# A four-layer transformer block on one core: the last layer's expert rows by inverted lists, its shared experts evicted by ScalarE and GpSimd, its experts chosen in turn

## What is computed

```python
def _gate(x2d, gate_w, gate_bias):                # E=16, K=4, G=4 groups, TG=2
    scores = jax.nn.sigmoid(x2d @ gate_w.T)
    sfc = scores + gate_bias[None, :]
    top2, _ = jax.lax.top_k(sfc.reshape(T, G, E // G), 2)
    _, gidx = jax.lax.top_k(top2.sum(-1), TG)     # the two best groups
    gmask = jnp.zeros((T, G), sfc.dtype).at[jnp.arange(T)[:, None], gidx].set(1.0)
    tmp = jnp.where(jnp.repeat(gmask, E // G, axis=1) > 0, sfc, 0.0)
    _, topk_idx = jax.lax.top_k(tmp, K)
    topk_w = jnp.take_along_axis(scores, topk_idx, axis=1)
    return (topk_idx, topk_w / (topk_w.sum(-1, keepdims=True) + 1e-20))
...
g = jnp.einsum('th,eih->tei', x, gate_proj)       # I=352 hidden units an expert
u = jnp.einsum('th,eih->tei', x, up_proj)
y = jnp.einsum('tei,ehi,te->th', jax.nn.silu(g) * u, down_proj, combine_w)
y = y + jax.nn.silu(x @ shared_gate_w.T) * (x @ shared_up_w.T) @ shared_down_w.T   # 2 x 352 units
...
x = x + jnp.tanh(g_ffn[3]) * _L3_ffn_ref(_layernorm(x, axis=-1), ...)
```

## Time and profile before

| | |
|---|---|
| median of 3 runs | 2774.49 us (2771.5 to 2775.27) |
| the profiled execution | 2772.54 us, its span 2770.7 us |
| mean granted TensorE clock | 0.927 |
| TensorE busy | 2361.6 us (85%) |
| VectorE busy | 1306.6 us (47%) |
| ScalarE busy | 890.4 us (32%) |
| GpSimd busy | 664.1 us (24%) |

### The profile page before, as it was taken

How to read it: one execution, slowest core, us unless ns; L and a number is a source line. 1 busy time by engine, 2 the same in 40 slices (tenths; PEclk the granted TensorE clock), 3 DMA queues, 4 the chain that set the end, 5 groups by cost and what they waited for, 6 DMA issues and landing times. The chain is left out here.

```text
span 2770.7 us, 31859 instructions
## 1 busy us (share of the span) xinstructions
PE 2361.6 (85%) x11410; PEld 1572.0 (57%) x11410; DVE 1306.6 (47%) x2786; ACT 890.4 (32%) x1996; POOL 664.1 (24%) x751
## 2 busy tenths in 40 slices
PE   6898978879688759996899989999988647999995
PEld 3454654546447647775444555444556524888873
DVE  5766256662646631112667445567444551333325
ACT  3444235452243222221456323465322110111110
POOL 3034231212202112221100122100121035332346
PEclk9989989999789779998999999999999668999997
DMA  9000000000000322221000000000000032666633
GB/s 361 2 1 1 0 1 1 1 1 1 8 0 22 134 94 99 97 96 64 1 16 1 1 1 0 1 1 1 1 1 1 0 122 97 217 222 232 224 129 117
DMA packets 59109, 164.13 MB, mean 59 GB/s; under 512 B 6529, under 2 KB 41089, under 8 KB 50913
## 3 DMA queue, kind: packets, MB, share of 16 engines
q0 software_dynamic: 20032, 90.00, 9.3%
q1 hardware_dynamic: 38960, 72.59, 7.5%
HBM read 119.84 MB, written 42.73 MB: 59 GB/s over the span
## 5 line engine op out<-in xcount | busy, mean ns | idle before, releaser
L646 ACT ACTIVATE arena<-PS,arena 128x512 f32<-128x512 f32 (+3 forms) x512 | 305.7, 605 | 202.6 <-DVE arena L689 172.2
L689 DVE TENSOR_REDUCE arena<-PS 128x1 f32<-128x512 f32 (+3 forms) x512 | 273.0, 583 | 136.0 <-PE PS L591 84.9
L585 PE MATMUL PS<-arena 64*128 64x512 f32 (+3 forms) x1024 | 292.7, 564 | 31.8 <-ACT arena L646 21.3
L297 POOL TENSOR_TENSOR arena<-arena 128x4 f32<-128x4 f32 x41 | 47.0, 1145 | 754.7 <-DVE arena L308 440.8
L2312 PE MATMUL PS<-arena 128*128 128x256 f32 (+2 forms) x1128 | 215.9, 348 | 0.9 <-DVE arena L2357 0.9
L2312 PEld LDWEIGHTS PS<-arena 128*128 128x128 f32 (+1 forms) x1128 | 182.3, 183 | 28.9 <-issue 1.3
L585 PEld LDWEIGHTS PS<-arena 64*128 64x128 f32 x1024 | 103.6, 186 | 144.0 <-ACT arena L646 95.6
L615 PE MATMUL PS<-arena 128*128 128x128 f32 x1280 | 170.7, 278 | 15.7 <-ACT arena L646 12.8
L870 POOL TENSOR_TENSOR arena<-arena 128x512 f32<-128x512 f32 (+2 forms) x108 | 88.8, 825 | 381.8 <-ACT arena L841 376.2
L615 PEld LDWEIGHTS PS<-arena 128*128 128x128 f32 x1280 | 137.4, 141 | 69.4 <-ACT arena L646 48.0
L982 PE MATMUL PS<-arena 128*128 128x512 f32 x384 | 168.0, 594 | 3.1 <-ACT arena L999 3.1
(11 more groups left out here) (395 smaller groups left out, 3932.4 us busy)
## 6 DMA issues: line engine op xcount, KB each, us to landing
arena<-e SPq DMA_DIRECT2D x8, 2048.0 KB, 8.6
slots<-zeros SPq DMA_DIRECT2D x1, 10112.0 KB, 60.8
arena<-slots SPq DMA_DIRECT2D x32, 256.0 KB, 3.3
yslots<-arena POOLq DMA_DIRECT2D x32, 256.0 KB, 2.6
arena<-w3a SPq DMA_DIRECT2D x1, 4106.0 KB, 13.6
yslots<-zeros SPq DMA_DIRECT2D x1, 4096.0 KB, 32.9
arena<-w3b SPq DMA_DIRECT2D x1, 3593.0 KB, 20.2
arena<-yslots SPq DMA_DIRECT2D x6, 512.0 KB, 5.8
```

What stands on the lines that cost most here:

```text
L585: ins = nc.tensor.matmul(PS[:, hh, 0:w], q[:, t * P:(t + 1) * P], k[:, 0:w], start=True, stop=not cfg["causal"])
L646: nc.scalar.activation(PRB[m % 6][:, 0:w], PS[:, hh, 0:w], ACT.Exp, bias=nmax[:, m:m + 1], accum_out=rsum[:, col:col + 1]).then_inc(s["pro ...
L689: nc.vector.tensor_reduce(nmax[:, m:m + 1], PS[:, hh, 0:w], AX, ALU.max, negate=True).then_inc(s["nmax"], 1)
```

## The change

It has five parts.

1. **Experts are chosen in turn.** `dve_take` replaces `dve_rank` for the experts of both mixtures: it takes the largest score (the first of equals), writes its one-hot mask, lowers it by a large number and goes on. That is six operations on 256 elements for each of the four choices (128 elements and two choices in the third layer). The mask of chosen experts is bf16.
2. **Places by products alone.** `pe_positions` lets TensorE add up the tiles before, with bf16 tables of ones (`ones16`, `upto16`); the running sums on VectorE are gone, in both mixtures.
3. **The fourth layer gets inverse lists** as the third has: one-hot rows of 64 x 79 and 64 x 128 elements (`dve_onehots3`), 64 products (`pe_rows3`) and `dve_rows3`. GpSimd gathers each tile of rows from the tokens by `from_row3` and stores each tile of outputs by `to_row3`; SyncE keeps the normalised tokens in `slots3`, reads a batch's expert number from `weight_row3` into a register and loads the weights by a plain DMA, and reads the outputs back by 16 plain DMAs. The 64 scatters, the 64 gathers and the 10 MB of zeros are gone.
4. **Shared experts** leave VectorE. ScalarE does silu and copies the up part and, scaled, the down part out of PSUM; GpSimd multiplies and adds to x. Gate and up of the next block stand ahead of the down products of a block. Half 0 starts when the scores are copied, and the two sets of products of the routing stand within it, behind its first and its last block; half 1 stays behind the batches. Its last four additions wait until VectorE has combined everything (`summed`), and the combining of a quarter waits for GpSimd's additions (`added`).
5. **The third layer's routing** also hands one multiplication of its one-hot rows to GpSimd (`pool_onehots`), and TensorE adds the parts for the second list. Empty slots read a row of zeros in `slots2`.

```diff
+            for k, (pick, top) in enumerate(zip(picks, tops)):
+                ch.link(v.tensor_reduce(top, val, AX, ALU.max))
+                ch.link(v.tensor_tensor(key, val, over(top), ALU.is_equal))
+                ch.link(v.scalar_tensor_tensor(out=key, in0=place, scalar=-float(P), in1=key, op0=ALU.add, op1=ALU.mult))
+                ch.link(v.tensor_reduce(least, key, AX, ALU.min))
+                ins = v.tensor_tensor(pick, key, over(least), ALU.is_equal)
...
+                ch.link(v.scalar_tensor_tensor(out=val, in0=pick, scalar=NEG, in1=val, op0=ALU.mult, op1=ALU.add))
...
+        def pool_onehots(highs, n, nh, signal):
+
+            for k in range(n // NT):
+                ins = nc.gpsimd.tensor_tensor(highs[:, k * NT:(k + 1) * NT, 0, :], highs[:, k * NT:(k + 1) * NT, 2, :],
+                                              counting[:, 1:NT + 1].unsqueeze(2).to_broadcast([P, NT, nh]), ALU.mult)
+            ins.then_inc(signal, 1)
+
+        def pe_positions(to, chosen, n, e):
+
+            for d in range(n):
+                ins = nc.tensor.matmul(to[:, d * e:n * e], ones16[:, :] if d else upto16[:, :], chosen[:, 0:(n - d) * e],
+                                       start=d == 0, stop=d == n - 1)
...
-            rank = temp(NT * E3).rearrange("p (t e) -> p t e", e=E3)
-            dve_rank(ch, sfc, rank, E3)
...
+            dve_take(ch, sfc, [onehot[:, k] for k in range(TOPK3)], TOPK3 * [top], E3)
...
-            V.tensor_copy(slot_of3[:, :], slot).then_inc(s["slots"], 1)
+            nseg = TOPK3 * NT
+            high, low = temp(nseg), temp(nseg)
+            dve_floor(ch, high, slot, P)
+            ch.link(V.scalar_tensor_tensor(out=low, in0=high, scalar=-float(P), in1=slot, op0=ALU.mult, op1=ALU.add))
+            dve_onehots3(ch, low3, high3, low, high, nseg, HI3, s["tables"])
...
             V.tensor_copy(weight_row3[:, :], row_).then_inc(s["slots"], 1)
+            v.wait_ge(s["table_psum"], 2)
+            dve_rows3(ch, PS[:, 3, 300:300 + 2 * HI3], HI3, TOPK3 * NT * P, from_row3[:, :], to_row3[:, :], temp,
+                      s["slots"])
...
+        def pool_mix3(pool, it, c):
+            n = IC3[c]
+            pool.wait_ge(s3m["up_out"], it * 6 + 2 * c + 2)
+            to = mixed3[it % 2][c][0:n, :]
+            nc.gpsimd.tensor_tensor(to, to, ups3[(it * 3 + c) % 2][0:n, :], ALU.mult).then_inc(s3m["mixed"], 1)
+
+        def pool_add3(pool, it):
+            for t in range(QT):
+                pool.wait_ge(s3m["down_out"], it * QT + t + 1)
+                xt = X[:, it % B * QT + t, :]
+                nc.gpsimd.tensor_tensor(xt, xt, downs3[t], ALU.add).then_inc(s3m["added"], 1)
...
+            for j in range(NB3):
+                jj, i = divmod(j, 3)
+                j_ = batch_expert(jj, i)
+                first = sp.value_load(weight_row3[0:1, j_:j_ + 1], min_val=0, max_val=(E3 - 1) * P)
+                if j >= 3:
+                    sp.wait_ge(s["o_psum"], j - 2)
+                elif j == 1:
+                    sp.wait_ge(s2m["kept"], KEPT2 + 32)
+                sp.dma_start(wbuf3[i], e3_in.rearrange("e p n -> (e p) n")[bass.ds(first, P), :]).then_inc(s[f"w{i}"], 16)
...
+            for q in range(B):
+                for k in range(TOPK3):
+                    sp.dma_start(yk3[:, k, q * QT:(q + 1) * QT, :], kept_rows(yslots3, k * NT + q * QT, QT)
+                                 ).then_inc(BACK3[q][0], 16)
...
             for q in range(B):
-                v.wait_ge(s[f"gathered{q}"], TOPK3 * QT * 16)
+                v.wait_ge(BACK3[q][0], BACK3[q][1] + TOPK3 * 16)
+                if q < B - 1:
+                    v.wait_ge(s["added"], (B + q + 1) * QT)
+                else:
+                    v.wait_ge(s["added"], B * QT)
...
+            def rows(j):
+                jj, i = divmod(j, 3)
+                if j >= 3:
+                    pool.wait_ge(s["xT_psum"], j - 2)
+                for t, n in enumerate(batch_tiles(jj, i)):
...
+            def store(j):
+                jj, i = divmod(j, 3)
+                pool.wait_ge(s["copied"], j + 4)
...
+            for j in range(NB3):
+                store(j)
+                if j + 3 < NB3:
+                    rows(j + 3)
+
+            def before_last():
+                pool.wait_ge(s["summed"], B * TOPK3)
+            pool_shared3(pool, 1, before_last)
...
-            sp.dma_start(slots3[0:ROWS3, :].rearrange("(t p) c -> p t c", p=P),
-                         zeros[:, :].unsqueeze(1).to_broadcast([P, ROWS3 // P, C])).then_inc(ld["zeroed"], 16)
```

More of the change, by code:

```diff
@@ L1624, in program @@
                    "y1_stored first back0 back1 back2 wa wb act_in hidden o_psum")
[L1625 to L1626 removed]
+        s3m = sems("l3moe", "sig tables table_psum slots x0 x1 x2 w0 w1 w2 xT_psum xT copied y0_stored y1_stored "
+                   "y2_stored back3 wa act_in dve_in hidden o_psum extra up_psum up_out mixed down down_out added summed")
         gtile = hT.rearrange("p a n -> p (a n)")
@@ new lines, in pool_shared3 @@
+        def pool_shared3(pool, i, last):
+            for b in range(B):
+                it = i * B + b
+                pool_mix3(pool, it, 0)
+                if b:
+                    pool_add3(pool, it - 1)
+                pool_mix3(pool, it, 1)
+                pool_mix3(pool, it, 2)
+            last()
+            pool_add3(pool, i * B + B - 1)
+        XN3 = region("kv", 0, NT * C).rearrange("p (t c) -> p t c", c=C)
+        wbuf3 = [region("kv", first, W3X) for first in (12544, 0, W3X)]
@@ L2273, in sp_moe3 @@
         def sp_moe3(sp):
             s = s3m
[L2277 to L2288 removed]
+            sp.wait_ge(s["slots"], 1)
@@ new lines, in store, with first_rows @@
+            def store(j):
+                jj, i = divmod(j, 3)
+                pool.wait_ge(s["copied"], j + 4)
+                for t, n in enumerate(batch_tiles(jj, i)):
+                    at_ = bass.IndirectOffsetOnAxis(ap=to_row3[:, n:n + 1], axis=0)
+                    nc.gpsimd.indirect_dma_start(out=yslots3, out_offset=at_, in_=ys3[i][:, t * C:(t + 1) * C], in_offset=None
+                                                 ).then_inc(s[f"y{i}_stored"], 16)
+            def first_rows():
+                pool.wait_ge(s2m["kept"], KEPT2 + 32)
+                pool.wait_ge(s["slots"], 2)
+                for j in range(3):
+                    rows(j)
```

434 lines of the change are left out of this document (207 added, 227 removed).

## The result

The changed kernel takes 2748.55 us (2746.07 to 2753.2), the kernel before 2772.99 beside it; the ratio is 0.9913, with a 95% interval of 0.9896 to 0.993. It is faster, as forecast, but by 0.9% where 3% were forecast, and the time lies above the range of 2664 to 2714.

What follows compares the result with a forecast made beforehand. The prediction took TensorE's own work plus three holes (58.9, 19.3, about 32 us) as the bound; terms of -100 and +15 for mutual hindrance gave -85 from 2772.5, 2687.5, on the median 2689.5 us, range 2664 to 2714.

Steps and rivals of the forecast that it cites:

- The start of the fourth layer: Fourth layer up to its first batch: shared expert 0 beside the routing, -68 us; -59 with GpSimd and VectorE hindering each other.
- GpSimd's hindrance: GpSimd and VectorE computing together: +9 us at the fourth layer's start, +3 in the third layer, +3 at the end.
- The mechanism of the hindrance: GpSimd beside VectorE: each operation waits for the rest of the instruction under way, not 0.2 us; together +15 us.
- TensorE not cold: First gate and up of the batches: 5.34 us instead of 7.95, -2.6 us; 0 if 3 us of rest cool it.
- The loop: The 47 batches: TensorE's work unchanged, second batch's gathers late behind stores, +2 us, bounds 0 and 16.
- the landing under load: Second row gather of a round in the batches: lands 4.6 us after issue; each us beyond costs one in 15 rounds.
- The rival of late gathers: Row gathers in the batches land at 6 to 6.5 us: +21 to +28 us, about 2714; chance 0.15.
- The end: Shared expert 1 to the end: plain DMAs replace GpSimd's gathers, -24.2 us, with +3 for GpSimd and VectorE hindering each other.
- The third layer: Third layer's routing up to its first gather: -7.3 us, with +3 for GpSimd's product behind VectorE's 4.42 us operation.
- They don't hinder each other: Rival: GpSimd and VectorE computing together cost each other nothing, 2674.5 us; chance 0.25.
- The relay binds: Rival: in shared experts ScalarE and GpSimd hold PSUM banks too long, blocks take 20 us for 16.1, 2720 us; chance 0.06.
- The fourth, slower than before: Rival: gathers in the batches land above 10.2 us in each of 15 rounds, giving back 85 us; chance 0.03.

Runs made afterwards that it cites:

- the memset run: Row gathers ahead of the stores in the changed kernel, and shared expert 0's GpSimd products and additions replaced by a one-column memset: 2680.43 us in one execution.
- the pieces: Changed kernel with VectorE's routing one-hot operations on 5056 and 8192 elements each made in eight pieces: 2750.39 us in one execution.
- the one-column run: Changed kernel with GpSimd's products and additions in shared expert 0 made on one column instead of 512 and 256: 2736.24 us in one execution.
- the small weights: Changed kernel with the weights of batches 3 to 46 cut from 2176 columns to 64: 2688.11 us in one execution.
- the first run: Changed kernel with row gathers of the batch three later put ahead of this batch's stores: 2688.67 us, 0.9705 of the kernel before.

## Why the prediction was wrong, step by step

**The start of the fourth layer: right.** -59 was the sum of the terms with GpSimd's hindrance, -58.2 was measured. Its parts hold too. Without hindrance the forecast had the first turning 76.5 us after the scores were copied; the memset run gives 75.7. The hindrance was put at 9 us and measured 10.5, by the way that was forecast: VectorE was to be held for 13 us with 4 of them swallowed, and in the changed kernel it wrote the weight rows 13.5 us later than in the memset run (75.5 after the copy for 62.1) and the first gather went out 9.9 later. Three ends of single steps, forecast and measured from the copy of the scores in the memset run: the weight rows 65.3 and 62.1; the list products 67.7 and 65.5; the first gather's issue 70.7 and 68.3. The one-hot rows were priced at 23.5 us and took 21.1, the blocks at 16.1 and took 15.5. (The working has the choice out at 2215.7 where its own terms give 2215.4; VectorE waits for TensorE there, so nothing hangs on it. GpSimd's share of a block, priced at 5.6 us, is 6.7 undisturbed, also off the path.) The landing gave it back: 7.5 us from the first gather's issue to the turning where 5.8 stood (8.1 in the changed kernel, with a hole of 8.3 us on TensorE ahead of the turning, over the 6 that the prediction named as a sign). The steps came 2.4 us early, the landing 1.7 late and the hindrance cost 1.5 more: that the sum is right to 0.8 us is in part luck.

**The mechanism of the hindrance: right.** I chose the bound by which a GpSimd operation waits for the rest of VectorE's instruction over the 0.2 us of the earlier trace rows. The runs show it: 13.6 us for three products, a single column that took 8.65 us beside an operation of 8.68, and a wait that shrinks with the pieces. The Trainium skill, page "SBUF — State Buffer", section "Who interferes with whom", calls the contention for the ports that VectorE and GpSimd share an exclusive lock; its words "fully blocks" stand at VectorE's two-port mode, and the prediction carried them over to the operations with two inputs. By the lock the choice was right, and the 8.65 us agree. The memset beside operations with two inputs, 0.10 us, also agrees with its saying that it is GpSimd's reading that contends.

**TensorE not cold: wrong, 2.6 us.** The first gate and up took 8.02 us, where the kernel before has 7.95. The prediction had allowed for it in a bracket, "0 if 3 us of rest cool it". The hole ahead was 8.3 us; in the one-column run it was 2.4 us, and the same products took 8.04.

**The loop: the step that failed.** The prediction found the place (the second batch of a round), the reason (rows asked for only behind the stores), the slack (4.6 us), and the rate (a us a round for each us of landing beyond that). It put the landing at 4.6, a single row, and bounded it with 1 us more. The first gather of the same pair, issued between 1048.5 and 1049, had taken longer in the kernel before:

```profile
arena<-slots,from_row POOLq DMA_INDIRECT x1, 5.5
```

In the changed kernel, the two gathers of the first round at that place:

```profile
arena<-slots,from_row POOLq DMA_INDIRECT x1, 4.7
...
arena<-slots,from_row POOLq DMA_INDIRECT x1, 7.1
```

The second is the one that TensorE waits for. 7.1 - 4.6 is 2.5 us. In all 14 rounds that gather landed in 6.1 to 8.0 us, 7.2 on average, and TensorE wanted it 4.6 to 4.7 us after its issue, so each landing was too late; the 14 waits average 2.6 and are 36.1 us for the 2 forecast. The step that failed is thus this one term, the landing under load, put at 4.6 us and measured at 7.2. A round took 24.2 us, over the 21 that the prediction had named as its sign of being wrong. The single row of the third layer was no measure of this loop. There one load of 2 MB serves two batches and was asked for 3.1 us ahead of these gathers. Here each batch brings 1.1 MB, and two loads are under way: in the first round one was asked for at 2309.2, 3.1 us ahead of the first gather, and one more at 2313.4, when the down products of the one-tile batch had ended, beside the second gather (2313.6). That the loads stretch the landing is shown by the small weights. How much of it is the second load is not, for in the first run, with the gathers asked for earlier, they landed in 6.1 us in the median all the same. The rival of late gathers had the right mechanism, at 6 to 6.5 us and a chance of 0.15; its 21 to 28 us were still too few. The range's upper end, at 2714, was put where that rival ended, and the 9.7 us of the earlier trace rows, the slowest landing at hand, would have carried it further: at 7.1 us the prediction's own rule gives +38.

**What no term had: the clock.** Each of the 14 waits is 1.5 to 3.5 us, and behind seven of them TensorE ran the next down products in part at the lower clock. Behind a wait of 2.50 us and one of 3.31 in the changed kernel:

```profile
2320.80 0.66 PE L2379 MATMUL PS<-arena 128*128 128x128 f32 x4 [2.50 <-DMA arena<-slots,from_row]
2321.29 2.76 PE L2406 MATMUL PS<-arena 128*128 128x256 f32 x12
...
2368.66 0.66 PE L2379 MATMUL PS<-arena 128*128 128x128 f32 x4 [3.31 <-DMA arena<-slots,from_row]
2369.15 4.44 PE L2406 MATMUL PS<-arena 128*128 128x256 f32 x12
```

Three of the seven followed waits over 3.3 us, the other four waits of 2.56 to 2.69, and one wait of 3.16 had none behind it, so these rows don't order by the length of the wait. Their seven rows sum to 29.8 us for 7 x 2.76, 10.4 us more. The rows of the turning products sum to 22.0 us for 19.7, 2.3 more, most of it in four of the same rounds. The last 2.3 of the 15.0 are no clock: where nothing stands between, a row's start overlaps the end of the one before by 0.16 us, and behind the 14 waits it doesn't. So the clock took some 12 us, a term nearly as large as the whole upper bound was. With the waits gone, in two different ways, it went as well.

**The end: right.** S + 74.8 for S + 75.5. GpSimd held VectorE: 16 additions took 8.9 us for 6.80 in each of the first two quarters, with single ones of up to 1.56 us where none of the kernel before is over 0.53. Only the last 32 additions lie on the path, 15.6 us for 13.6, so 2 us where 3 stood. Besides, TensorE's four blocks took 63.7 us, not 64.4, and the last store and the end 4.7 for 3.3.

**The third layer: -6.0 for -4.3.** The prediction put 3 us on the path for the product that stands behind the 4.42 us operation; the lists started 0.9 us later than with the product on VectorE, 2.4 later than if it had been free (0.9 and the 1.5 of the product). That accounts for 0.6 of the 1.7 us; the rest was not placed.

**The rivals.** "They don't hinder each other" falls with the memset run. "The relay binds" falls as well: the blocks took 15.5 us, and TensorE's only waits for it are the 4.15 us of the blocked product and 1.16 in the last block of shared expert 1. The fourth, slower than before, needed landings over 10.2 us; the changed kernel's longest was 8.0.

## What to carry to other kernels

When a change ties a transfer's issue to an event, ask what else that event releases and what else is in flight then: a single landing from another loop is no measure of this one, and the range should go to the slowest landing at hand. In a loop that an engine fills completely, ask for the inputs of the batches to come before storing the outputs of this one, as soon as their buffer is free; here it cost nothing and was worth 51 us. And before giving arithmetic to GpSimd beside VectorE, look how long VectorE's instructions with two inputs are there, since each of GpSimd's may wait for a whole one. Cutting them lets GpSimd in but has a price of its own.

## What of the hardware was not expected

- A GpSimd operation that multiplies one column takes 0.19 us alone and took 8.65 us beside a VectorE operation of 8.68 us with two inputs: 10.8 us for four and 10.3 us for three. A GpSimd memset beside the same VectorE operations takes 0.10 us.
- A GpSimd memset stood 1.42 us beside a VectorE bf16 operation with one tensor input and a scalar operand (5056 elements in 1.59 us), and ended with it. It is a single case. The Trainium skill, same page and section, says that a tensor_scalar can enter a two-port mode, and that VectorE in such a mode contends with GpSimd; this case agrees, and no run here tried it apart.
- An indirect gather of 128 rows of 1 KB lands in 2.8 us (median of 74) with little else on the DMA engines and in 6.1 us (median of 76) beside loads of 1.1 MB, at 214 GB/s in all; holding such loads back until the first rows had landed made these land 3 to 4 us sooner.
- With 14 waits of TensorE of 1.5 to 3.5 us, one in each 22 to 26 us, its mean granted clock over 382 us was 0.96; with none it was 0.99, in two runs that took them away in different ways.
